# Two key blocks of the causal diagonal in one attention step: 288 steps in place of 320

## The reference, cut to what matters

```python
qkv = x @ w_qkv
q, k, v = jnp.split(qkv, 3, axis=-1)              # to (B, 16 heads, 2048, 64)
q = _apply_rope(q, cos, sin)
k = _apply_rope(k, cos, sin)
scores = jnp.einsum('bhqd,bhkd->bhqk', q, k) * scale
causal = jnp.tril(jnp.ones((S, S), dtype=bool))
scores = jnp.where(causal, scores, jnp.finfo(scores.dtype).min)
attn = jax.nn.softmax(scores, axis=-1)
out = jnp.einsum('bhqk,bhkd->bhqd', attn, v)
...
x = _layernorm(x + attention(x), axis=-1)
gate = jax.nn.silu(_bitlinear(x, w_gate))
up = _bitlinear(x, w_up)
x = _layernorm(x + _bitlinear(gate * up, w_down), axis=-1)
```

## Time and profile before

| what | value |
|---|---|
| time before, median of 3 runs | 1223.97 us (1222.83 to 1224.78) |
| the profiled execution: its time | 1223.76 us |
| its span, first to last instruction of core 2, the slowest | 1222.2 us |
| spans of the 8 cores | 1214.8 to 1222.2 us |
| PE busy, whole span | 1157.6 us (95%), 6470 matmuls |
| ACT busy | 665.6 us (54%) |
| DVE busy | 701.5 us (57%) |
| POOL busy | 125.0 us (10%), 217 instructions |
| the chain that ended last, by engine | PE 76%; ACT 12%; DMA 6%; POOL 3% |

### The profile page before, as it was taken

How to read it: one execution, slowest core, us unless ns; L and a number is a source line. 1 busy time by engine, 2 the same in 40 slices (tenths; PEclk the granted TensorE clock), 3 DMA queues, 4 the chain that set the end, 5 groups by cost and what they waited for, 6 DMA issues and landing times.

```text
span 1222.2 us, 17266 instructions; the slowest of 8 cores (1214.8 to 1222.2 us)
## 1 busy us (share of the span) xinstructions
PE 1157.6 (95%) x6470; PEld 493.4 (40%) x6470; DVE 701.5 (57%) x999; ACT 665.6 (54%) x847; POOL 125.0 (10%) x217
## 2 busy tenths in 40 slices
PE   3898999999999988999999999999999999999998
PEld 1343333333333322344444444444444444444443
DVE  2369866676676843478884544554544544543343
ACT  4236899998998987644445245235344344343400
POOL 3011134132332231000000000000000000000000
PEclk9998999999999999899999999999999999999999
DMA  9999999966999785457786344344344333332482
GB/s 281 314 322 335 271 283 321 306 215 180 287 325 316 254 277 156 146 158 220 224 206 147 95 119 115 78 121 121 75 120 116 78 95 112 69 99 74 103 161 73
DMA packets 152705, 225.22 MB, mean 184 GB/s; under 512 B 107888, under 2 KB 112112, under 8 KB 137264
## 3 DMA queue, kind: packets, MB, share of 16 engines
q1 hardware_dynamic: 148784, 214.28, 60.2%
q0 software_dynamic: 3840, 9.84, 2.8%
HBM read 148.19 MB, written 46.53 MB: 159 GB/s over the span
## 4 chain that ended last, share of the span: by engine, by line
PE 76%; ACT 12%; DMA 6%; POOL 3%; DVE 1%; issue 1%; DVEq 0%; SPq 0%; ACTq 0%
PE sc L851 36%; PE av L915 16%; ACT E L632 9%; PE pj L401 6%; PE sc L621 5%; PE pj L770 5%; DMA ring<-wg 4%; PE av L654 4%; PE su L654 3%; PE sc L915 2%; POOL E L637 2%; DMA ring<-xu 2%; ACT Rb L676 1%; ACT Lb L674 1%; ACT QK L411 1%
## 5 line engine op out<-in xcount | busy, mean ns | idle before, releaser
L632 ACT ACTIVATE E<-sc,cst 128x1024 bf16<-128x1024 f32 (+1 forms) x320 | 301.8, 987 | 42.3 <-PE sc L621 40.8
L861 ACT ACTIVATE sg<-sc,st 128x512 bf16<-128x512 f32 x128 | 87.8, 686 | 306.5 <-PE sc L851 285.8
L851 PE MATMUL sc<-TG,xqT 128*128 128x512 fp8e4 x1024 | 241.9, 379 | 0.0
L851 PE MATMUL sc<-TU,xqT 128*128 128x512 fp8e4 x1024 | 241.9, 379 | 0.0
L915 PE MATMUL av<-TD,hqT 128*128 128x512 fp8e4 x896 | 195.7, 379 | 0.0
L867 DVE TENSOR_TENSOR h<-sc,sg 128x512 f32<-128x512 f32 x128 | 88.3, 690 | 163.0 <-PE sc L851 140.9
L401 PE MATMUL pj<-xT,wqk 128*64 128x512 bf16 (+1 forms) x928 | 149.9, 400 | 23.2 <-DVE xT L354 20.9
L851 PEld LDWEIGHTS sc<-TG,xqT 128*128 128x128 bf16 x1024 | 100.2, 98 | 120.8
L851 PEld LDWEIGHTS sc<-TU,xqT 128*128 128x128 bf16 x1024 | 100.2, 98 | 120.8
L621 PE MATMUL sc<-QK,QK 64*128 64x512 bf16 (+3 forms) x640 | 117.2, 361 | 22.6 <-ACT E L632 19.1
L915 PEld LDWEIGHTS av<-TD,hqT 128*128 128x128 bf16 x896 | 87.7, 98 | 105.7
(11 more groups left out here) (87 smaller groups left out, 887.2 us busy)
## 6 DMA issues: line engine op xcount, KB each, us to landing
ring<-wg SPq DMA_DIRECT2D x28, 1024.0 KB, 19.4
ring<-wu SPq DMA_DIRECT2D x28, 1024.0 KB, 11.9
ring<-wd SPq DMA_DIRECT2D x16, 1024.0 KB, 8.4
dstg<-wd SPq DMA_DIRECT2D x16, 1024.0 KB, 7.0
hqs<-hq SPq DMA_DIRECT2D x64, 256.0 KB, 2.7
ring<-wqk SPq DMA_DIRECT2D x8, 1024.0 KB, 12.8
ring<-xu SPq DMA_DIRECT2D x8, 1024.0 KB, 25.7
swp<-QK POOLq DMA_DIRECT2D x64, 128.0 KB, 8.3
```

The costliest lines, as they stand in the source:

```text
L632: t2 = act.do(lambda e: e.activation(Et[:, :, lo:512], out[:, :, lo:512], AF.Exp, bias=c_(4), scale=0.125), t, *more)
L851: fn = lambda e, kc=kc, dst=dst, W=W: e.matmul(dst, x_[:, kc, :], W[:, n, kc * 512:(kc + 1) * 512], start=(kc == 0), stop=(kc == 7))
```

## The change

The last two key blocks of a query block, r = 2 and r = 3, become one step. `steps` now has 36 entries for a pair and 288 in all. `parts_of` gives the parts of a step as (key block, first query column, place in the tile); the merged step has two, (kc, 256, 0) and (kc + 1, 384, 256). Its scores fill columns 0 to 383 of each bank: 256 from the first key block and 128 from the second. One exponential covers both (2 x 384 = 768 elements per partition), and one mask covers the first 128 columns of both parts in both heads (512 elements). `attend` of the merged step puts on PE first both parts' matmuls with V, then both parts' matmuls with ones. The numbers of matmuls and of their columns are what they were.

Three numbers that pace other work by steps are changed with it: `nfill` grows by 2.7 and 1.78 a step in place of 2.4 and 1.6, and `bgrate` divides by `nstep - 52` in place of `nstep - 58`. LAG, NE, the delays of `later`, and stages 1, 3 and 4 stay.

```diff
--- before.py
+++ after.py
@@ -588,7 +588,17 @@
         SC = [t.rearrange("p (a b) -> p a b", a=2) for t in SC]
         LAG = 3
         NE = 5
-        steps = [(c, j, kc) for c in range(NP) for j in range(4) for kc in range(4 * j + 4)]
+        steps = [(c, j, kc) for c in range(NP) for j in range(4) for kc in range(4 * j + 3)]
+        def parts_of(s):
+            c, j, kc = steps[s]
+            if kc == 4 * j + 2:
+                return [(kc, 256, 0), (kc + 1, 384, 256)]
+            lo = max(0, kc - 4 * j) * 128
+            return [(kc, lo, lo)]
         nstep = len(steps)
         t_exp = {}
         t_av = {}
@@ -603,37 +613,43 @@
         for c in range(1, NP):
             fill += pair_proj(c)
         bgdone = 0.0
-        bgrate = len(seq) / float(nstep - 58)
+        bgrate = len(seq) / float(nstep - 52)
         blk = {"n": 0}
         t_lastsc = None
 
         def scores(s):
             c, j, kc = steps[s]
-            r = kc - 4 * j
-            lo = 128 * r if r > 0 else 0
             Q, Kt = QK[c % 3]
             out = SC[s % 2]
             toks = [t_rope[(c, 0)], t_rope[(c, 1)], t_exp.get(s - 2)]
             if s < 2:
                 toks += [vb_free[2 * s], vb_free[2 * s + 1]]
-            for hh in range(2):
-                p0 = hh * 64
-                fn = lambda e, p0=p0, hh=hh: e.matmul(
-                    out[:, hh, lo:512], Kt[p0:p0 + 64, kc * 128:(kc + 1) * 128],
-                    Q[p0:p0 + 64, j * 512 + lo:(j + 1) * 512], start=True, stop=True)
-                if hh == 0:
-                    pe.quiet(fn, *toks)
-                else:
-                    t = pe.do(fn)
+            ps = parts_of(s)
+            for k, lo, at_ in ps:
+                for hh in range(2):
+                    p0 = hh * 64
+                    fn = lambda e, p0=p0, hh=hh, k=k, lo=lo, at_=at_: e.matmul(
+                        out[:, hh, at_:at_ + 512 - lo], Kt[p0:p0 + 64, k * 128:(k + 1) * 128],
+                        Q[p0:p0 + 64, j * 512 + lo:(j + 1) * 512], start=True, stop=True)
+                    if hh == 1 and k == ps[-1][0]:
+                        t = pe.do(fn)
+                    else:
+                        pe.quiet(fn, *toks)
+                        toks = []
             Et = E[s % NE]
             more = [t_av.get(s - NE)]
             if s < NE:
                 more += [t_tabw]
-            t2 = act.do(lambda e: e.activation(Et[:, :, lo:512], out[:, :, lo:512], AF.Exp,
+            a, z = ps[0][2], ps[-1][2] + 512 - ps[-1][1]
+            t2 = act.do(lambda e: e.activation(Et[:, :, a:z], out[:, :, a:z], AF.Exp,
                                                bias=c_(4), scale=0.125), t, *more)
             t_exp[s] = t2
-            if r >= 0:
-                tri = Et[:, :, lo:lo + 128]
+            if len(ps) == 2:
+                tri = Et.rearrange("p a (b q) -> p a b q", q=256)[:, :, :, 0:128]
+                t2 = pool.do(lambda e: e.affine_select(tri, tri, [[0, 2], [0, 2], [1, 128]], ALU.is_ge, 0.0,
+                                                       base=0, channel_multiplier=-1), t2)
+            elif kc >= 4 * j:
+                tri = Et[:, :, a:a + 128]
                 t2 = pool.do(lambda e: e.affine_select(tri, tri, [[0, 2], [1, 128]], ALU.is_ge, 0.0,
                                                        base=0, channel_multiplier=-1), t2)
             t_E[s] = t2
@@ -642,28 +658,29 @@
         def attend(s):
             c, j, kc = steps[s]
             n = 4 * c + j
-            sp_ = kc == 4 * j + 3
-            for what, q in ((0, s), (1, s - 1), (1, s)) if kc == 1 else ((0, s),) if kc == 0 else ((0, s), (1, s)):
-                cq, jq, kq = steps[q]
-                rq = kq - 4 * jq
-                lq = 128 * rq if rq > 0 else 0
-                for hh in range(2):
-                    dst = (AV[n % 2], SU)[what][hh * 64:(hh + 1) * 64, lq:512]
-                    w = (V[:, kq, (2 * c + hh) * 64:(2 * c + hh + 1) * 64], onesb)[what]
-                    fn = lambda e, hh=hh, w=w, dst=dst, q=q, lq=lq, kq=kq: e.matmul(
-                        dst, w, E[q % NE][:, hh, lq:512], start=kq == 0, stop=sp_ and q == s)
-                    toks = []
-                    if what == 0 and hh == 0:
-                        toks = [t_E[s], t_V[(kc, c // 4)], t_onb]
-                        if kc == 0:
-                            toks += [av_free[n % 2]]
-                    if what == 1 and hh == 0 and kq == 0:
-                        toks = [su_free]
-                    if what == 1 and hh == 1:
-                        t_av[q] = pe.do(fn)
-                    else:
-                        pe.quiet(fn, *toks)
+            sp_ = kc == 4 * j + 2
+            todo_ = [(0, s)] if kc == 0 else [(0, s), (1, s - 1), (1, s)] if kc == 1 else [(0, s), (1, s)]
+            for what, q in todo_:
+                ps = parts_of(q)
+                for k, lo, at_ in ps:
+                    for hh in range(2):
+                        dst = (AV[n % 2], SU)[what][hh * 64:(hh + 1) * 64, lo:512]
+                        w = (V[:, k, (2 * c + hh) * 64:(2 * c + hh + 1) * 64], onesb)[what]
+                        end = sp_ and q == s and k == ps[-1][0]
+                        fn = lambda e, hh=hh, w=w, dst=dst, q=q, k=k, lo=lo, at_=at_, end=end: e.matmul(
+                            dst, w, E[q % NE][:, hh, at_:at_ + 512 - lo], start=k == 0, stop=end)
+                        toks = []
+                        if what == 0 and hh == 0:
+                            toks = [t_E[s], t_V[(k, c // 4)], t_onb]
+                            if k == 0:
+                                toks += [av_free[n % 2]]
+                        if what == 1 and hh == 0 and k == 0:
+                            toks = [su_free]
+                        if what == 1 and hh == 1 and k == ps[-1][0]:
+                            t_av[q] = pe.do(fn)
+                        else:
+                            pe.quiet(fn, *toks)
             if sp_:
                 finish_block(c, j, n, t_av[s])
 
@@ -1048,7 +1065,7 @@
                     if c > 0:
                         qk_free[(c - 1) % 3] = t_lastsc
                 t_lastsc = scores(s)
-                nfill += 2.4 if c == 0 else 1.6
+                nfill += 2.7 if c == 0 else 1.78
                 while fill and nfill >= 1:
                     if s == skip:
 
```

## The result

The kernel with the change takes 1207.15 us at the median (1206.47 to 1207.89, 4 runs) against 1223.43 for the kernel before on the same chip (4 runs): a ratio of 0.9855, 95% interval 0.9812 to 0.9898. The profiled execution took 1206.47 us, with a span of 1204.9 us on core 0, the slowest. Executions in which all cores of a die ran at a lower clock took 2% or more longer, and all times and ratios here leave them out.

The account below looks back on a forecast made before the run. PE and ACT, both nearly full beside fill with PE the fuller, were taken as the coupled bound. 5.4 + 0.85 + 1.3 - 0.5 = 7.05 us less than 1223.76 gave 1216.8 us, range 1210 to 1225.

Parts of the forecast that it names:

- PE's passages: Switches between kinds of matmul in scores and `attend`: 0.20 us less per query block, 5.4 us over 27 blocks with fill.
- The bound of -0.20: Far end for PE: weight loads of the eight short `attend` matmuls worked one behind the other, a loss of 0.20 us per block.
- The rule quoted from the Trainium skill: Merged scores on PE: a weight load overlaps running matmuls only where the row group is another, so second loads stand free.
- The rival that rested on the rule: No gain on PE: weight loads stand free, 5.4 us falls away and about 1.6 stays, 1222 us; chance 0.14.
- The fill that moves: Fill comes in fewer, larger portions between steps; costed at nothing, or 2 us in all if ACT led.
- Waits close as well: Rival: ACT no longer runs dry at each diagonal, half of PE's 11.1 us behind exponentials goes too, 1211 us; chance 0.14.
- the saved 0.27 us: One exponential of 768 elements in place of 512 and 256: 0.27 us less on ACT, no second gain beside fill.
- ACT's 39% of the chain: ACT's share of the waits from 250 to 320 us; its shrinking lets the chain follow PE, whose share is about 60%.
- the blocks without fill: Five query blocks where ACT leads: 0.17 us less each, 0.85 us in all.
- POOL at the start of the last pair: Masks queued while DVE copies `wo`: 1.5 us less in the queue, PE's wait taken to fall by 1.3 us.
- Lateness: The merged mask is done 0.73 us later after its scores; taken as 0.5 us lost in all, bounds 0 and 7.3.
- The clock: Lower-clock stretches behind PE's waits in the last pair: one more or less is 1 to 2 us either way.

Follow-up runs that it names:

- fill_as_before: The changed kernel with the fill at its old places, the merged step taking the portions of both steps it replaces: 1219.17 us, 0.9956 of the kernel before.
- two_exps: The changed kernel with the merged step's exponential split again into 512 and 256 elements: 1212.08 us, 0.9895 of the kernel before.
- pe_order_alone: The changed kernel with two exponentials, two masks and the old fill places, so only PE's matmul order is merged: 1220.81 us, 0.9965 of the kernel before.
- two_passages: The changed kernel with the r = 1 scores cut in two from query block 1 on, attend's `av` matmuls between: 1211.75 us, 0.9887 of the kernel before.
- threshold_later: The changed kernel with each FFN weight's threshold work asked for 8 steps behind its last sum, not 3: 1211.4 us, 0.9902 of the kernel before.

## Why the prediction was wrong

The direction and the first mechanism were right, the size was not. By the steps of the prediction:

- **PE's passages: right, and a little small.** I took 0.20 us of an upper value of 0.22 a block; the timeline shows 0.27, and pair 1's busy time 0.30. The scores save 0.12 where I had 0.10, `attend` 0.15 where I had 0.12. But the term was multiplied by 27 blocks. Pair 0's four gave nothing; 23 blocks at 0.27 are 6.2 us, against the 5.4 forecast: that the two agree so nearly is luck, since the blocks were miscounted. The bound of -0.20 did not come true. The rule quoted from the Trainium skill, "TensorE: Matmul & The Clock Gate", Part 3, is not borne out in this kernel: scores of 256 and 128 columns on the same rows passed in 0.26 us up to the fill, and nothing of the loads was exposed. The same Part of the Trainium skill also lets a load into the background weight buffer go ahead, which the prediction left out. And the trace before did have a sequence to judge it by: fill matmuls follow each other on all 128 rows, with a load of 109 ns between them, at 0.22 us an item, no more than their columns. The rival that rested on the rule is out, and its 0.14 was too high for that reason.
- **The fill that moves: "I cost it at nothing". This is the step that failed.** The argument was that PE is the fuller engine, so that a long portion makes ACT wait and not PE. The first fact was right; the conclusion wasn't. PE was idle for 2.9 of 48.8 us in a filled pair, because it ran dry in single steps, and where the fill stands decides how often. `fill_as_before` differs from the change in the places alone, and takes 7.0 us more in pairs 1 to 5 (5.9 undisturbed). Without the new places the merge gains 5 us, somewhat less than the 7 forecast.
- **The waits between PE and ACT.** "Waits close as well" was the rival nearest to what came, at 5.5 us more than the forecast and with a chance of 0.14. PE's idle time fell by 1.0 us in pair 1 and by 4.3 in pairs 1 to 5 (16.2 to 12.0 at the median core). Its reason was wrong: not the shorter exponentials (`two_exps` has the same pairs) but PE's merged order and the fill that goes with it. `pe_order_alone` shows that the order with the old fill places even raises the waits, by 0.5 us in pair 1.
- **ACT.** That the saved 0.27 us is no second gain beside fill agrees with the pairs of `two_exps`; about 1 us of its total stays unexplained. The reason that I gave, that ACT's 39% of the chain had to shrink for PE's gain to count, falls with the same run. For the blocks without fill I had 0.85 us; `two_exps` gives back 0.9 in the four of pair 7, on cores without a lower-clock stretch. That size was right.
- **POOL at the start of the last pair: 1.3 forecast, about 0.8 found**, the 1.8 and 1.0 us that leaving the masks out saved, with the clock in both. Lateness was too small at 0.5: waits for masks in pairs 1 to 5 did fall, from 3.8 to 3.1 us, but masks lengthen these pairs by 1.5 us in the change and by 0.1 before.
- **The clock: "1 to 2 us either way".** In the kernel before all eight cores have a lower-clock stretch in pair 7, five in pair 3, one in pair 2 and one in pair 5; after the change one core has any in pair 7 and none in pairs 1 to 6. In pair 3 of the kernel before the five cores take 51.2 to 51.3 us and the others 50.1, so a stretch is 1.1 us there. Nearly all of them went one way, where I had left the sign open (the repeat of the change has one in pair 5 and some on two cores in pair 7); that shorter waits are the reason is argued, not shown. In pair 7 the clock may be most of the 2.5 us: the least disturbed core of before takes 54.0 us there, the undisturbed ones of the change 52.5.

The sum by the runs, for a middle core: passages 6.2 (5.4 of them in pairs 1 to 5), idle time 4.3 and clock 1.0 in pairs 1 to 5, 0.4 more in pair 6, pair 7 2.5, pair 0 nothing: 14.4 us. The slowest core gained 17.3, since the slowest of before, core 2, had lower-clock stretches in pairs 3, 5 and 7. How much of a pair's 1.0 us of idle time belongs to the merge and how much to the places can't be split by a sum: the merge without the places raises idle time, and the places without the merge bring POOL's issues in the way. With one placing rule for both kernels pair 1 is idle for 2.82 us with 320 steps and for 1.42 with 288, so under that rule it goes with the merge.

## What to carry to other kernels

- When two engines are both nine tenths busy and coupled step by step, a change of the steps also moves the filler, and the filler's places are a term of the sum and not a detail: price the idle time of the fuller engine (here 2.9 us a pair) as what may be won or lost, and try the new steps and the new places apart and together.
- A busy share tells which engine leads on average; whether it waits is decided in single steps. An instruction removed from the other engine (ACT's exponential) was worth little or nothing in the trace where filler was at hand, and about its length where there was none.
- Faster steps bring late data forward: look in the stretches that gained nothing for a wait whose partner is a load or another engine, as in pair 0.

## What the runs showed of the hardware

- A passage of PE between matmuls of unlike shape on its array (scores on 64 rows, `av` on 64 columns) cost 0.1 us each with the columns unchanged: in `two_passages` pair 1 is 47.2 us on all eight cores in place of 46.6, for three there-and-backs; the two more score matmuls of each and their loads are in that price.
- A mask of twice the elements took 649 ns against 407: 0.95 ns an element and about 165 ns fixed. Beside DVE's work single masks took up to 1.6 us, and two DMA issues on POOL 2.57 us in one place against 0.99 in another.
- In the kernel before, 1.47 us of waiting in pair 3 (line 540, for an ACT copy) stands in a stretch with a granted clock of 0.97; the change's pair 3 has the same matmul with 1.2 us of waiting and 1.00 throughout. With 1.8 us in `threshold_later` six of eight cores have the lower clock there. The length of the wait does not decide it alone: all eight cores of the kernel before have the same wait, and three of them kept 1.00 in that pair.
